# Graph network on one core: the gate column moves from VectorE to ScalarE

## The reference, cut to what matters

```python
h = relu(layernorm(x))
edge_input = concatenate([h[src], edge_attr])              # 96 + 32 features
messages = gelu(edge_input @ mW1 + mb1) @ mW2 + mb2
gates = sigmoid(gelu(edge_input @ gW1 + gb1) @ gW2 + gb2)  # one number per edge
aggregated = segment_sum(messages * gates, dst)
update = gelu(concatenate([h, aggregated]) @ uW1 + ub1) @ uW2 + ub2
x = x + layernorm(h + update) * ln_g + ln_b
# then two graph convolutions with gated residuals over the same edges
```

## Time and profile before

| | us |
|---|---|
| Median of three runs | 8850.81 |
| The profiled execution (its own time, the span of its trace) | 10933.0 |
| Edge stage in it, from the first gather L962 to the end of the last segment sum | 5657.9 |
| Convolution stage in it, from the first to past the last gather L1007 | 4805.9 |
| The rest of it (set-up, node update, end) | 469.2 |

### The profile page before, as it was taken

One profiled execution on the slowest core, in us unless ns is written; L12 is line 12 of the kernel. 1 busy time (PEld: TensorE's weight loads), 2 busy tenths in 40 slices (PEclk: granted clock), 3 DMA queues, 4 the chain that ended last, 5 costly groups with the idle time before them and its releaser, 6 DMA issues. The chain is left out here.

```text
span 10933.0 us, 150076 instructions
## 1 busy us (share of the span) xinstructions
PE 8192.3 (75%) x42144; PEld 5220.9 (48%) x42144; DVE 4899.6 (45%) x11836; ACT 2690.1 (25%) x6600; POOL 6435.5 (59%) x6424
## 2 busy tenths in 40 slices
PE   4777777777777777777777578887777577887776
PEld 4555555555555555555555233333334333433333
DVE  7666666666666666666667122222222121222222
ACT  3444444444444444444443000000000000000000
POOL 4555555555555555555554666666664666666663
PEclk7888888888888888888887788888887688888887
DMA  4444444444444444444444456666565465666656
GB/s 147 123 138 131 136 132 136 132 135 132 135 133 135 133 135 135 134 135 133 135 132 134 155 207 220 216 218 214 208 212 198 156 215 206 224 217 210 210 207 207
DMA packets 933049, 1818.03 MB, mean 166 GB/s; under 512 B 277359, under 2 KB 745600, under 8 KB 875312
## 3 DMA queue, kind: packets, MB, share of 16 engines
q10 hardware_dynamic: 65600, 773.65, 18.6%
q1 hardware_dynamic: 615456, 578.39, 16.9%
q0 software_dynamic: 251856, 464.10, 14.8%
HBM read 1361.12 MB, written 454.48 MB: 166 GB/s over the span
## 5 line engine op out<-in xcount | busy, mean ns | idle before, releaser
L962 POOL DMA_INDIRECT hid<-src_table,src_ids x3127 | 3136.7, 1003 | 2510.4 <-ACT msg L1358 1590.2
L1240 PE MATMUL bd<-ring,table_sb 128*96 128x480 f32 x6272 | 2941.6, 614 | 513.3 <-issue 511.7
L1240 PEld LDWEIGHTS bd<-ring,table_sb 128*96 128x96 f32 x6272 | 1071.7, 176 | 2131.6 <-issue 2131.1
L1007 POOL DMA_INDIRECT hid<-conv_table,hid x1596 | 1561.9, 979 | 751.1 <-issue 486.2
L1155 PE MATMUL sg<-hot,msg 128*98 128x64 f32 x6272 | 831.1, 286 | 1115.9 <-ACT msg L1358 1105.2
L1132 PE MATMUL bd<-one_hot_dst,one_hot_src 128*128 128x168 bf16 (+1 forms) x10368 | 1277.0, 274 | 253.5 <-issue 252.3
L1007 POOL DMA_INDIRECT feat_in<-conv_table,hid x1056 | 1026.1, 972 | 545.2 <-issue 324.6
L1155 PEld LDWEIGHTS sg<-hot,msg 128*98 128x98 f32 x6272 | 746.8, 199 | 1252.2 <-issue 1180.0
L1972 DVE TENSOR_TENSOR acc<-acc,sg 96x64 f32 x400 | 87.2, 218 | 2450.0 <-remote 1652.7
L1132 PEld LDWEIGHTS bd<-one_hot_dst,one_hot_src 128*128 128x128 bf16 x10368 | 1007.1, 110 | 299.1 <-issue 284.3
L1367 ACT ACTIVATE blocks<-bd 128x480 f32<-128x480 f32 (+1 forms) x1152 | 658.1, 571 | 1704.7 <-PE bd L1132 811.8
(11 more groups left out here) (248 smaller groups left out, 10307.8 us busy)
## 6 DMA issues: line engine op xcount, KB each, us to landing
ring<-adjacency ACTq DMA_DIRECT2D x448, 1680.0 KB
adjacency<-blocks SPq DMA_DIRECT2D x384, 980.0 KB
attr<-in_attr SPq DMA_DIRECT2D x392, 128.0 KB
hid<-src_table,src_ids POOLq DMA_INDIRECT x3127
hid<-conv_table,hid POOLq DMA_INDIRECT x1596
feat_in<-conv_table,hid POOLq DMA_INDIRECT x1056
conv_table<-table_sb SPq DMA_DIRECT2D x28, 336.0 KB, 2.4
feat_half<-feat_keep SPq DMA_DIRECT2D x56, 168.0 KB
```

What stands on the lines that cost most here:

```text
L962: pool.indirect_dma_start(out=hid[s][:, t, :], out_offset=None, in_=src_rows, in_offset=bass.IndirectOffsetOnAxis(ap=src_ids[h][:, j:j + 1 ...
L1007: pool.indirect_dma_start(out=conv_g[j][slot][:, t, :], out_offset=None, in_=conv_rows[l], in_offset=bass.IndirectOffsetOnAxis(ap=conv_ids ...
L1240: op = nc.tensor.matmul(side_ps[w].rearrange("r (o z) -> r o z", o=UNIT_OCTETS), table_sb[:, D * k:D * (k + 1)], ring[slot][:, :, OCTET_FA ...
```

## The change

Three things are changed. The instruction that makes the gate column is taken off DVE and issued by ACT, at the head of `weigh`: an Identity activation with scale 0.5 and a bias column that holds 0.5. POOL fills that bias column once at the start. ACT now waits for its own `s_tanh` and for the release of the `msg` buffer (`s_seg`) before it, and for its completion (`s_gcol`) before the four multiplications. DVE's `gate` ends with the weight column and signals a new semaphore `s_hot` there; it waits for tanh no more. PE waits for `s_hot` and `s_gated`. `tanh` may overwrite its buffer once the gate column two quads back has been made (`s_gcol`) rather than once that quad has been weighed (`s_gated`).

```diff
-POOL_CONSTANTS = 12
+POOL_CONSTANTS = 13
@@
+        half = sb("half", [P, 1])
@@
+        s_hot = sem("slots_and_weights")
@@ POOL's set-up
+                         lambda: pool.memset(half[:, :], 0.5),
@@ PE, edges
+                    pe.wait_ge(s_hot, QUADS_PER_ITER * n + s + 1)
                     pe.wait_ge(s_gated, QUADS_PER_ITER * n + s + 1)
@@ ACT
             def tanh(n, s, free):
                 act.wait_ge(s_dotted, QUADS_PER_ITER * n + s + 1)
                 if free:
-                    act.wait_ge(s_gated, QUADS_PER_ITER * n + s - 1)
+                    act.wait_ge(s_gcol, QUADS_PER_ITER * n + s - 1)
@@
-            def weigh(n, s):
-                act.wait_ge(s_gcol, QUADS_PER_ITER * n + s + 1)
+            def weigh(n, s, free):
+                i = QUADS_PER_ITER * n + s
                 m = msg[s % 2]
+                act.wait_ge(s_tanh, i + 1)
+                if free:
+                    act.wait_ge(s_seg, i - 1)
+                nc.scalar.activation(m[:, :, GATE_ROW], gate_t[s % 2][:, :], ACT.Identity,
+                                     bias=half[:, 0:1], scale=0.5).then_inc(s_gcol, 1)
+                act.wait_ge(s_gcol, i + 1)
@@
-                    weigh(n, s)
+                    weigh(n, s, not (first and s < 2))
@@ DVE, gate
-                v.tensor_copy(m[:, :, DEG_ROW], weight[:, bass.ds(it * TILES_PER_ITER + QUAD * s, QUAD)])
-                dve.wait_ge(s_tanh, i + 1)
-                v.tensor_scalar(m[:, :, GATE_ROW], gate_t[s % 2][:, :], 0.5, 0.5, ALU.mult, ALU.add).then_inc(s_gcol, 1)
+                v.tensor_copy(m[:, :, DEG_ROW],
+                              weight[:, bass.ds(it * TILES_PER_ITER + QUAD * s, QUAD)]).then_inc(s_hot, 1)
```

## The result

The changed kernel takes 8792.05 us (median of 4 runs, 8788.90 to 8797.95), the kernel before 8850.6 us beside it: ratio 0.993, interval 0.9918 to 0.9942. The prediction said 8861 and gave "faster" 0.24; the change is faster by 0.7%.

A forecast was written before the change was run, and what follows sets the result against it. POOL's gathering was taken to set the pace of the timed runs. The ACT instruction added 11 us and the other terms 0, so 8851 + 11 = about 8861 us; own range 8833 to 8869, over all rivals 8790 to 8975.

The forecast's parts named there:

- faster: The outcome that DVE sets the pace and the change gains time, at first price 8788 us; chance 0.24.
- The 390 waits of PE and the late signals of the earlier trace: Edge stage: PE waits 1105.2 us for the weighing, every second quad; PE's signal comes 4.3 us after the matmuls' recorded end.
- rival A: Edge stage: the new ACT instruction delays PE's chain 0.33 us every second quad; full price +129 us, 8980 us; chance 0.35.
- DVE's wait for tanh: Edge stage: 371.8 us in 158 cases go, but DVE then waits for the segment sum anyway; priced at 0.
- PE's new wait: PE's wait for `s_hot`: its instruction stood ahead of the gate column, for which PE waited anyway; priced at 0.
- the term on the gathers: POOL's edge gathers: their length taken as unchanged, so DVE's saved 63 us lies behind them; priced at 0.
- rival C: Edge stage: fewer DVE instructions let POOL's gathers run quicker, 15 us, so 8836; inside the forecast's chance of 0.41.
- the 8667: Least time POOL's gathers allow: edges 4075, convolutions 4069, outside both 469, between convolutions 54; the median lies 184 us above.
- Rival B: Edge stage: DVE sets the pace; 0.08 us less per quad gives -63, 8788 us, down to 8700; chance 0.24.
- The term for the ACT instruction: New instruction ahead of the weighing: 0.33 us per quad, +129 us in the profiled execution, +11 us in timed runs.
- The premise on the profile: The profiled execution spans 2082 us more than the timed median; most of its edge waits cannot be in timed runs.
- scaling them to 8.3%: Edge stage: 132 us of the 184 above POOL's least time, against 1590 us of POOL's waits in the trace.

The follow-up runs named there:

- the earlier trace: Kernel before, unchanged, in its first profiled execution, taken to be of the slower chip's kind; span 10933.0 us.
- the spare instruction with it: Changed kernel with one more DVE tensor_scalar of 128x4 per quad, behind the weight column and waiting for tanh first; 8817.1 us, 0.9974 of the kernel before.
- The spare instructions: One more 128x4 instruction per quad: on the changed kernel's DVE, tensor_scalar 8827.0, reduce 8824.91, memset 8801.21 us; on ACT in the kernel before, 8816.68.
- before, again: Kernel before, unchanged, run and profiled once more at the faster level; 8842.79 us, span 8841.0 us.
- the piece on single kinds: Kernel before with ten times 16 gathers added at its end, one kind of DVE instruction running beside each set; 9128.39 us.
- ACT's instruction alone: Kernel before with one more 128x4 ACT Identity activation per quad ahead of the weighing, nothing taken from DVE; 8816.68 us, 0.9973 of the kernel before.
- the spare tensor_scalar: Changed kernel with one more DVE tensor_scalar of 128x4 per quad behind the weight column, without a wait; 8827.0 us, 0.9983 of the kernel before.
- the spare reduce: Changed kernel with one more DVE tensor_reduce of 128x4 per quad behind the weight column; 8824.91 us, 0.9972 of the kernel before, at the faster level.
- the other one-hot form: Kernel before with its 128x688 one-hots made by tensor_tensor instead of tensor_scalar; 8723.62 us. The same edit on the changed kernel: 8748.43 us.

## Why the prediction was wrong

**Where it was right.** POOL's gathering sets the pace of the timed runs: one gather less per quad takes off 609 us. The 390 waits of PE and the late signals of the earlier trace rows were no part of the timed runs (60.8 us in 10 cases), so rival A had nothing to multiply. The new instruction takes 292 ns as taken from tanh, and the weighing starts 0.32 us after it. DVE's wait for tanh is worth nothing (the spare instruction with it is 10 us faster than without). PE's new wait shows in no row that I read.

**The step that failed.** It is the term on the gathers. The sum took their length as fixed: what DVE saves "lies behind POOL's gathers: 0 in my sum", and what it might do to them came in only as rival C, at "784 of them would be 15 us". The gathers' sum fell by 63 us and the run by 59, and so the forecast of a hidden change at 8861 was wrong. The mechanism, fewer DVE instructions and quicker gathers, was on the list, and the mean against the median of the earlier trace rows was the row that showed it; but I divided the excess evenly over all 8882 DVE instructions. At the faster level the excess over 0.946 is larger, 3235.3 - 3127 x 0.946 = 277 us, and it hangs on few kinds and on when they run. (So POOL's least time was larger too: the edge gathers take 99 us more than the 3136.7 that went into the 8667, over half of the 184 us above it.) The spare instructions show that "one instruction less" isn't the unit: the same 128x4 kind that costs a gather nothing by itself costs 25 to 42 us when it is put into the queue, another on ACT gains 27, and a second one less on DVE gains nothing.

What changed is which gathers meet which instruction. I went through the timelines from 600 to 4200 us and noted, for each gather, which of the long kinds DVE was running 0.6 us after its start. Each cell: so many gathers, their mean, and what they lie above 0.946 us in sum, scaled to 3127 gathers.

| 0.6 us into the gather DVE runs | before, again | after |
|---|---|---|
| product, tensor_tensor 128x384 f32 | 308, 1.219, 98 us | 236, 1.182, 64 us |
| scalar_tensor_tensor 128x384 | 516, 1.077, 78 us | 507, 1.034, 51 us |
| one-hot, 128x688 | 219, 1.145, 51 us | 215, 1.148, 50 us |
| none of these | 1644, 0.972, 51 us | 1761, 0.971, 52 us |

The first two rows carry the gain, 61 us; the others stand still. The sorting is rough, to some 5 us a cell, and a row holds its instruction's neighbours too: under the 128x688 tensor_scalar a gather takes 1.145 us here and 0.982 in the piece on single kinds. The same count puts product, scalar_tensor_tensor, one-hot and rest at 77, 60, 65 and 47 us with ACT's instruction alone, at 93, 57, 60 and 51 with the spare tensor_scalar, at 83, 65, 57 and 53 with the spare reduce, and at 0, 142, 4 and 2 in the kernel before with the other one-hot form, where no gather meets a product at that moment any more (they start at 0.64, just behind it, and these gathers take 1.009 on average; with a product that starts 0.3 us in it is 1.198 in before, again). Two gathers of before, again show how it goes:
```profile
2502.15 0.60 DVE L1709 SCALAR_TENSOR_TENSOR one_hot_src<-iota_lo,side_now 128x384 bf16<-128x384 bf16 x1
2502.37 1.20 POOL L962 DMA_INDIRECT hid<-src_table,src_ids  x1 [0.30 <-issue]
2502.68 0.55 DVE L1671 TENSOR_TENSOR prod<-hid,gate_w 128x384 f32<-128x384 f32 x1
2503.26 0.55 DVE L1674 TENSOR_REDUCE buf_h<-prod 128x4 f32<-128x384 f32 x1
2503.73 0.95 DVE L1662 TENSOR_TENSOR hid<-pa,hid 128x768 f32<-128x768 f32 x1
2503.88 0.95 POOL L962 DMA_INDIRECT hid<-src_table,src_ids  x1 [0.31 <-issue]
```
The gather at 2502.37 starts under a scalar_tensor_tensor with a product behind it, and takes 1.20 us; the one at 2503.88 starts under the addition L1662, which reads PSUM, and takes 0.95. In the changed kernel, at the same kind of place:
```profile
2503.73 0.60 DVE L1718 SCALAR_TENSOR_TENSOR one_hot_src<-iota_lo,side_now 128x384 bf16<-128x384 bf16 x1
2504.23 0.95 POOL L965 DMA_INDIRECT hid<-src_table,src_ids  x1 [0.30 <-issue]
2504.26 0.38 DVE L1717 TENSOR_SCALAR one_hot_dst<-iota_z,side_now 128x688 bf16<-128x688 f16 x1
2504.57 0.60 DVE L1718 SCALAR_TENSOR_TENSOR one_hot_src<-iota_lo,side_now 128x384 bf16<-128x384 bf16 x1
2505.10 0.54 DVE L1681 TENSOR_TENSOR prod<-hid,gate_w 128x384 f32<-128x384 f32 x1
2505.48 0.98 POOL L965 DMA_INDIRECT hid<-src_table,src_ids  x1 [0.30 <-issue]
```
Here the product starts 0.87 us into the gather at 2504.23 and is over 0.16 us into the next, and neither is lengthened much. (The first has a scalar_tensor_tensor from 0.34 us on and takes 0.95 all the same, so the moment alone does not decide for that kind.) That the gain is in the gathers' length is shown by the traces, and that DVE can lengthen a gather by the piece on single kinds. That the change works by the shift is argued: the counts say so, and the spare instructions fit it, but no run set the shift by itself.

**Rival B** (8788 us) has the measured number by chance: its 784 x 0.08 us is DVE's own time on the path. The spare tensor_scalar alone would fit it, since it adds 49 us to DVE's busy time and costs 25 to 42. Three others do not: ACT's instruction takes nothing from DVE and gains 27 us, the weight column on ACT takes 58 us from DVE and gains nothing, and the slower one-hots add 434 us and gain 126. The 27 us with three gathers per quad are no proof of it either, since the gathers got shorter there too.

**The term for the ACT instruction**, +11 us, had the wrong sign: alone it gives -27. The Trainium skill ("ScalarE: Activation LUTs", Rules for kernel authors) gives a multiply or an add to VectorE, since it does it faster. For the instruction itself the trace agrees, 211 ns on DVE and 292 on ACT. For the kernel it does not carry over: with the slower one it is 0.7% faster, since neither engine's time is the limit.

**The premise on the profile.** I took the 2082 us between the profiled execution and the timed runs for a cost of recording. The recording costs nothing; the execution took the time of the other level. The timed runs' waits could not be read from the earlier trace rows, and scaling them to 8.3% was as good as leaving them out.

**The box that I named with rival C** (the Trainium skill, "SBUF — State Buffer", the box on "DVE blocks DMA") says that GpSimd cannot write a DMA's descriptors while DVE runs certain instructions. That a gather can be held up wholly agrees with 23.50 and 28.68 us for one, though it lasted to the end of a row of 50 or 35 and not of one instruction. The box names a plain f32 copy as a trigger; here 100 such copies of 128x384 leave the gathers at 0.958 us, and the kinds that hold one up have two tensor operands.

**Open.** Why a row of column-broadcast tensor_tensor blocks a gather wholly, while the same form in the edge stage (863 ns each, alone between others) leaves room and even gains 126 us; why two operands are not enough, since 71 gathers of before, again had the destination one-hot L1682 (a tensor_tensor with both operands in SBUF) at 0.6 us and took 0.948; the gap of 254 us on the slower chip; and what the change itself is worth there, where POOL waits 1590 us for the weighing and rival A has something to act on.

## What to carry to other kernels

Where POOL's indirect gathers set the pace, compare their mean with their shortest and look in the timeline at which DVE instruction runs beside the long ones: in this kernel 277 us of 8841 lie there, three times what POOL waits for the weighing. Then a small edit on DVE or ACT can move the time by 0.3 to 0.7%, up or down, without its own cost telling which, so such a gain is to be measured, not added to others. The form change of the one-hots helped both kernels, and the lowest time of a full kernel here (8723.6 us) has it, without the change that this document is about. And before a profile's waits are priced, check that its span agrees with the timed runs.

## What the runs showed of the hardware

- A gather of 128 rows keeps POOL busy 0.946 us with 0.30 us to the next. Under unbroken scalar_tensor_tensor or column-broadcast tensor_tensor on DVE one gather lasted to the end of the row of them (23.50 and 28.68 us), and 0.8 us longer. Under f32 tensor_tensor it is 1.10 us; under tensor_scalar, tensor_reduce, copy and memset 0.95 to 0.98.
- It goes both ways: DVE's 128x688 tensor_scalar takes 0.39 us at 2510.93 in before, again, beside the start of a gather, and 0.53 at 2501.70, 0.63 us into one:
```profile
2501.07 0.99 POOL L962 DMA_INDIRECT hid<-src_table,src_ids  x1 [0.30 <-issue]
2501.70 0.53 DVE L1708 TENSOR_SCALAR one_hot_dst<-iota_z,side_now 128x688 bf16<-128x688 f16 x1
...
2510.91 0.95 POOL L962 DMA_INDIRECT hid<-src_table,src_ids  x1 [0.30 <-issue]
2510.93 0.39 DVE L1708 TENSOR_SCALAR one_hot_dst<-iota_z,side_now 128x688 bf16<-128x688 f16 x1
```
- The same kernel takes about 8845 us on three chips and 10,925 on a fourth, with a granted TensorE clock of 0.92 and 0.84. Which is the cause of which is not shown.
